# A fused token-mixing, attention and feed-forward kernel on one core: ACT takes a normalisation and four copies, and DVE's and POOL's queues are re-ordered

## The reference

```
q, k, v = token mixing of x inside groups of 16 tokens (Wq, Wkv, biases), 8 tokens out
h = q*scale + softmax(q*scale @ k) @ v                       # (64, 128, 192)
h = h + attention(layernorm(h))    # 12 heads, 3 key/value heads, 64 wide, rope, softmax, Wo
h = h + gelu(layernorm(h) @ W_in.T + b) @ W_out              # 768 hidden
```

## Time and profile before

| | |
|---|---|
| time, median of 3 runs | 1117.43 us (1113.86 to 1119.33) |
| the profiled execution: its own time, its span | 1116.1 us, 1114.3 us |
| busy: PE, DVE, ACT, POOL | 985.3, 797.4, 654.4, 699.8 us |
| share of the span: PE, DVE, ACT, POOL | 88%, 72%, 59%, 63% |
| mean granted TensorE clock | 0.969 of full |

### The profile page before, as it was taken

One profiled execution on the slowest core, in us unless ns is written; L12 is line 12 of the kernel. 1 busy time (PEld: TensorE's weight loads), 2 busy tenths in 40 slices (PEclk: granted clock), 3 DMA queues, 4 the chain that ended last, 5 costly groups with the idle time before them and its releaser, 6 DMA issues. The chain is left out here.

```text
span 1114.3 us, 25412 instructions
## 1 busy us (share of the span) xinstructions
PE 985.3 (88%) x7360; PEld 843.2 (76%) x7360; DVE 797.4 (72%) x1935; ACT 654.4 (59%) x2402; POOL 699.8 (63%) x1063
## 2 busy tenths in 40 slices
PE   3678999999999999999999999999999999999877
PEld 2557778887777887877778787788787787878765
DVE  2677777778778777877777767877777777787751
ACT  2336655665665566566557566556566655756651
POOL 0566576666667666666766656766666676666660
PEclk7779999999999999999999999999999999999998
DMA  5043433344443334444333444333434333443331
GB/s 171 20 132 114 139 96 114 102 124 128 131 130 96 118 97 133 122 137 122 96 108 108 134 125 126 96 118 96 139 120 139 111 107 107 111 139 120 120 105 31
DMA packets 139936, 127.69 MB, mean 115 GB/s; under 512 B 30480, under 2 KB 123024, under 8 KB 139920
## 3 DMA queue, kind: packets, MB, share of 16 engines
q1 hardware_dynamic: 137632, 124.29, 37.5%
q10 hardware_dynamic: 2288, 3.21, 0.8%
HBM read 70.83 MB, written 56.62 MB: 114 GB/s over the span
## 5 line engine op out<-in xcount | busy, mean ns | idle before, releaser
L302 ACT ACTIVATE E<-ring,m_neg 128x128 f32<-128x128 f32 x768 | 271.1, 401 | 13.8 <-DVE m_neg L507 13.8
L402 POOL TENSOR_TENSOR E<-E,e_rcp 128x512 f32<-128x512 f32 x192 | 200.7, 1052 | 95.2 <-DVE e_rcp L527 92.5
L394 POOL TENSOR_TENSOR qkT<-rot_c,rot_s 128x256 f32<-128x256 f32 x256 | 188.1, 735 | 20.1
L518 DVE STREAM_TRANSPOSE EB<-E 128x512 f32<-128x512 f32 x192 | 134.5, 700 | 75.0 <-POOL E L402 75.0
L302 ACT ACTIVATION_READ_ACCUMULATOR E<-ring,m_neg 128x1 f32 x768 | 184.8, 241 | 0.0
L689 PE MATMUL bank<-wout_sb,G 128*128 128x192 f32 x768 | 147.8, 330 | 2.6 <-ACT G L367 2.6
L836 PE MATMUL ring<-wo_sb,OT 128*128 128x192 f32 x768 | 139.4, 332 | 10.4 <-ACT OT L310 10.4
L392 POOL TENSOR_TENSOR rot_s<-rot_s,rope_qs 128x256 f32<-128x256 f32 x192 | 141.0, 734 | 10.8 <-DVE rot_s L495 10.8
L836 PEld LDWEIGHTS ring<-wo_sb,OT 128*128 128x128 f32 x768 | 126.7, 192 | 24.4 <-issue 24.4
L689 PEld LDWEIGHTS bank<-wout_sb,G 128*128 128x128 f32 x768 | 125.3, 192 | 4.3 <-ACT G L367 3.1
L507 DVE TENSOR_REDUCE m_neg<-ring 128x4 f32<-128x512 f32 x192 | 125.6, 682 | 2.2 <-PE ring L708 2.2
(11 more groups left out here) (130 smaller groups left out, 2610.1 us busy)
## 6 DMA issues: line engine op xcount, KB each, us to landing
spill<-EB SPq DMA_DIRECT2D x64, 512.0 KB, 2.7
ET<-spill SPq DMA_DIRECT2D x256, 128.0 KB, 2.8
spill<-EB SPq DMA_DIRECT2D x64, 256.0 KB, 2.0
ET<-spill SPq DMA_DIRECT2D x256, 64.0 KB, 2.3
x_sb<-in_x_dram SPq DMA_DIRECT2D x64, 192.0 KB, 2.5
out_dram<-out_sb SPq DMA_DIRECT2D x64, 96.0 KB, 2.3
x_sb<-in_x_dram SPq DMA_DIRECT2D x64, 64.0 KB, 2.2
w_raw<-in_w_att_dram ACTq DMA_DIRECT2D x2, 608.0 KB, 5.2
```

What stands on the lines that cost most here:

```text
L302: last = nc.scalar.activation(E[:, a, s * P:(s + 1) * P], RING[a][:, s * P:(s + 1) * P], ACT.Exp, bias=m_neg[:, a, s:s + 1], accum_out=e_s ...
L394: nc.gpsimd.tensor_tensor(qkT[:, b, :, a], rot_c[:, b, :, a], rot_s[:, b, :, a], ALU.add).then_inc(q_out, 1)
L402: nc.gpsimd.tensor_tensor(e, e, r, ALU.mult).then_inc(prob_out, 1)
L518: nc.vector.transpose(EB[:, a, s0 * P:(s0 + heads) * P].rearrange("p (j h c) -> p h j c", j=NB, h=heads)[:, h0:h0 + REP], E[:, a, 512 * g: ...
```

## The change

ACT writes `hn` of sequence 0 at the start of its step, as rs * h2 + off, with off = -mean * rs from one more small POOL instruction (`off2`). ACT also makes the four copies `h_cur[0]`, `h_wait`, `v_late` and `h_cur[1]` that POOL made. In DVE's queue `normalise(..., 0)` is gone; `h_next` and its statistics stand ahead of the first block transpose; the residual sum and statistics of sequence 1 stand behind the first block transpose and ahead of the second; two of the three `key_max(1)` banks stand behind the `HL` and result instructions. In POOL's queue the last rotation precedes the first `probs`, and `ve1`/`rs1` precede `probs(0, 2)`, which still precedes `rstd2(..., 1)`. On PE `probs_v(0)` stands ahead of `x_turned`, and on ACT `heads_out(0)` ahead of `XH`.

```diff
 # ACT
+                if ffn:
+                    act.wait_ge(ln2_off, p)
+                    need(act, hT_mm, p - 1)
+                    nc.scalar.activation(hn[:, 0, 0:D], h2[:, 0, :], ACT.Identity, scale=rs2[:, 0:1], bias=off2[:])
+                    nc.scalar.activation(hn[:, 0, D:DP], h2[:, 0, P:D], ACT.Identity, scale=rs2[:, 0:1],
+                                         bias=off2[:]).then_inc(hn_out[0], 1)
+                if att:
+                    act.wait_ge(h_out, p + 1)
+                    need(act, h2_out, 2 * p - 1)
+                    nc.scalar.copy(h_cur[0][:], h_next[:, 0, :]).then_inc(h_kept[0], 1)
+                    nc.scalar.copy(h_wait[:], h_next[:, 1, :]).then_inc(h_moved, 1)
...
                     score_exp(0, 2)
+                    act.wait_ge(v_out, p + 1)
+                    need(act, pv_mm, 4 * p)
+                    nc.scalar.copy(v_late[:], v_tok[:, 1]).then_inc(v_kept, 1)
+                    act.wait_ge(h_moved, p + 1)
+                    need(act, h2_out, 2 * p)
+                    nc.scalar.copy(h_cur[1][:], h_wait[:]).then_inc(h_kept[1], 1)
...
                         score_exp(1, k)
+                    heads_out(0, p)
                 if tok:
                     act.wait_ge(xT_mm, n + 1)
...
-                if att:
-                    heads_out(0, p)
 # POOL
+                    if a == 0:
+                        wait_apart(pool, pool_passed, (ln2_rs, done))
+                        nc.gpsimd.tensor_scalar(off2[:], mv2[:, a, 0:1], rs2[:, a:a + 1], -1.0,
+                                                ALU.mult, ALU.mult).then_inc(ln2_off, 1)
...
-                    for i in range(3):
+                    for i in range(4):
                         rotated(1, i, i + 5)
-                    (copies h_cur[0], h_wait)
                     probs(0, 0, p)
-                    rotated(1, 3, 8)
                     probs(0, 1, p)
-                    probs(0, 2, p)
-                if ffn:
-                    rstd2(2 * p, 1)
                 if tok:
                     (ve1, rs1)
                 if att:
-                    (copies h_cur[1], v_late)
+                    probs(0, 2, p)
+                if ffn:
+                    rstd2(2 * p, 1)
 # DVE
-                    normalise(h2, mv2, rs2, hn, 0).then_inc(hn_out, 1)
...
                     sums_inverted(0, 0, p)
-                    blocks_turned(0, 0, p)
-                    sums_inverted(0, 1, p)
                 (h_next, its bn_stats)
+                if att:
+                    sums_inverted(0, 1, p)
                 (its bn_aggr)
+                if att:
+                    blocks_turned(0, 0, p)
                 if ffn:
                     dve.wait_ge(h_kept[1], p)
                     attention_added(1, 2 * p)
+                    attention_stats(1, 2 * p)
                 if att:
                     blocks_turned(0, 1, p)
                     sums_inverted(0, 2, p)
-                if ffn:
-                    attention_stats(1, 2 * p)
-                if att:
                     blocks_turned(0, 2, p)
                 (normalise sequence 1)
-                    key_max(1, (0, 1))
+                    key_max(1, (0,))
                 (HL, ffn_result)
-                    key_max(1, (2,))
+                    key_max(1, (1, 2))
 # PE
                     ffn_first()
+                if att:
+                    probs_v(0, p)
                 if tok:
                     x_turned()
                 if att:
-                    probs_v(0, p)
                     output(0, p)
```

More of the change, by code:

```diff
@@ L150, in program @@
         st2, mv2, ve2, rs2 = sb("st2", [P, 2, 6]), sb("mv2", [P, 2, 2]), sb("ve2", [P, 2]), sb("rs2", [P, 2])
-        hn = sb("hn", [P, 2, DP])
+        hn, off2 = sb("hn", [P, 2, DP]), sb("off2", [P, 1])
         HH, HL = sb("HH", [P, 2, 2, P], F32R), sb("HL", [P, 2, 2, P], F32R)
@@ L184, in program @@
         y_mm, h2_out, h2_copied = sem("y_mm"), sem("h2_out"), sem("h2_copied")
-        ln2_st, ln2_mv, ln2_ve, ln2_rs, hn_out = (
-            sem(n) for n in ("ln2_st", "ln2_mv", "ln2_ve", "ln2_rs", "hn_out"))
+        ln2_st, ln2_mv, ln2_ve, ln2_rs, ln2_off = (
+            sem(n) for n in ("ln2_st", "ln2_mv", "ln2_ve", "ln2_rs", "ln2_off"))
+        hn_out = [sem("hn_out0"), sem("hn_out1")]
         hT_mm, HH_out, HL_out = sem("hT_mm"), sem("HH_out"), sem("HL_out")
@@ L409, in step @@
                         rotated(0, i, i + 1)
-                    for i in range(3):
+                    for i in range(4):
                         rotated(1, i, i + 5)
-                    wait_apart(pool, pool_passed, (h2_out, 2 * p - 1), (h_out, p + 1))
-                    nc.gpsimd.tensor_copy(h_cur[0][:], h_next[:, 0, :]).then_inc(h_kept[0], 1)
-                    nc.gpsimd.tensor_copy(h_wait[:], h_next[:, 1, :]).then_inc(h_moved, 1)
                     probs(0, 0, p)
-                    rotated(1, 3, 8)
                     probs(0, 1, p)
-                    probs(0, 2, p)
-                if ffn:
-                    rstd2(2 * p, 1)
                 if tok:
@@ L530, in attention_added @@
                     dve.wait_ge(y_mm, done)
+                    if a == 0:
+                        need(dve, hn_out[0], (done - 1) // 2 if isinstance(done, int) else p)
                     nc.vector.tensor_tensor(h2[:, a, :], ATT_Y, h_cur[a][:], ALU.add).then_inc(h2_out, 1)
@@ L560, in step @@
                     v_out_of_psum()
-                if ffn:
-                    dve.wait_ge(ln2_rs, 2 * p - 1)
-                    need(dve, hT_mm, p - 1)
-                    normalise(h2, mv2, rs2, hn, 0).then_inc(hn_out, 1)
                 if tok:
@@ L592, in step @@
                                             ALU.add).then_inc(h_out, 1)
-                if tok:
                     dve.wait_ge(h_out, n + 1)
@@ L596, in step @@
                         nc.vector.bn_stats(st1[:, a, :], h_next[:, a, :]).then_inc(ln1_st, 1)
+                if att:
+                    sums_inverted(0, 1, p)
+                if tok:
                     wait_apart(dve, dve_passed, (ln1_st, 2 * n + 2))
@@ L611, in step @@
                     dve.wait_ge(ln2_rs, 2 * p)
-                    normalise(h2, mv2, rs2, hn, 1).then_inc(hn_out, 1)
+                    need(dve, hT_mm, p - 1)
+                    normalise(h2, mv2, rs2, hn, 1).then_inc(hn_out[1], 1)
                 if att:
-                    key_max(1, (0, 1))
+                    key_max(1, (0,))
                 if ffn:
@@ L814, in hn_turned @@
                 def hn_turned():
-                    pe.wait_ge(hn_out, 2 * p)
+                    pe.wait_ge(hn_out[0], p)
+                    pe.wait_ge(hn_out[1], p)
                     if tok:
```

## The result

The changed kernel takes 1099.13 us (median of 4 runs, 1095.57 to 1100.08). The kernel before takes 1115.99 us over its 4 runs of the same comparison. The ratio is 0.984, with a 95% interval of 0.9805 to 0.9876: 1.6% faster. The profiled execution took 1100.08 us, its span is 1098.3 us.

A forecast was written before the change was run, and what follows sets the result against it. PE's own work plus its waits for t_a, hn and output(0) bound the step. 0.34 + 0.34 - 0.12 = 0.56 us, 16.2 us in 29 steps plus 0.3 in the drain, gave 1100.9; predicted 1100.5, range 1091 to 1112.

The forecast's parts named there:

- my sum: Whole kernel: 0.56 us a step, 16.2 us in 29 steps, giving 1100.9 us to compare; chance 0.50.
- t_a and the mask add: Front of the step: DVE's mask add 0.6 us earlier at most, t_a 0.56; PE's 0.43 us wait for t_a goes.
- The DVE distances: Middle of DVE's queue: 3.74 us from h_next to sums_inverted(0, 2); hn starts 2.14 us after that reciprocal.
- The gain at hn: Middle of the step: hn of sequence 1 comes 0.34 us earlier; PE's wait for it grows from 1.58 to 1.67 us.
- my ceiling of 2.35 us a step: PE's three idle times, before t_a, hn and output(0): the most the change can win, 68 us in 29 steps.
- Its cause: DVE: h_next, no longer behind sums_inverted(0, 1), waits for tok_h instead; sums_inverted(0, 2) starts 0.35 us earlier.
- output(0), 0.34 us: End of the step on PE: x_turned fills the wait for ACT's copy of OT before output(0), winning 0.34 us.
- The gelus, 0.12 us: ACT's gelus become late, so PE waits 0.09 to 0.15 us at the token-mixing products; taken as 0.12.
- The ET reload: Before the second half of probs_v(0) on PE: the reload lands with about 0.3 us of slack, so it is free.
- The clock: PE's granted clock: five of 29 steps stay at reduced clock, each losing 1.3 us.
- The slower rival: The longer wait before the hn transposes lets PE's clock fall every step: 31 us more, 1132 us; chance 0.08.
- The weak side: POOL: sequence 1's statistics come a microsecond earlier, but rstd2 still cannot pass probs(0, 2).

The follow-up runs named there:

- e5: Changed kernel with eight x_sb products first on PE and the gelu wait moved behind them, ahead of the four x2_sb products; 1093.39 us, ratio 0.9803.
- e1: Kernel before with only hn of the first sequence moved from DVE to ACT (off2 on POOL), all orders and POOL copies kept; 1101.09 us, ratio 0.9824.
- e3: Changed kernel with the middle of DVE's and POOL's queues put back in the old order; 1096.39 us, ratio 0.9768.
- e9: e3 with e5's late wait for the gelus; 1092.48 us, ratio 0.9787.
- e4: Changed kernel with only the end order put back: x_turned ahead of probs_v(0) on PE, heads_out(0) behind XH on ACT; 1103.7 us, ratio 0.9851.
- e6: e5 with rstd2(1) ahead of probs(0, 2) on POOL and the second sequence's normalisation ahead of the third block transpose on DVE; 1067.23 us, ratio 0.9569.
- e10: e9 with e6's edit to rstd2 on POOL and the normalisation on DVE; 1119.12 us, ratio 1.0012.
- e7: Changed kernel with one more unused 192-column copy on POOL ahead of rstd2 of the second sequence; 1121.66 us, ratio 1.0058.
- e11: e6 with rstd2(1) also ahead of ve1 and rs1 on POOL; 1086.53 us, ratio 0.9722.
- e8: Changed kernel with one more unused 192-column copy on ACT right ahead of the gelu table load; 1106.05 us, ratio 0.9904.

## Why the prediction came out right, and where its steps did not

The time, 1099.1 us against 1100.5 (my sum gave 1100.9), and the step, 0.53 us less against 0.56, were right. Most of the terms were not.

- **t_a and the mask add.** Right. With the gelu stop out of the way (e5) the add stands at 10.52 in the step against 11.13, the 0.6 us of the sum.
- **The DVE distances.** Right: 3.78 us measured for 3.74, and 2.13 us for 2.14 from there to `hn`.
- **The gain at hn, 0.34 us.** Too small. PE's `hn` transposes stand at 22.53 in e5 against 22.96, 0.43 us. I had taken the stop for `t_a` at the 0.43 us of idle time; `tok_h` on PE moved by 0.57 us (14.97 against 15.54 in e5). A stop of PE costs more than the idle time in its row, so my ceiling of 2.35 us a step was too low as well. PE is ready for `hn` 0.72 us earlier (20.66 in e5 against 21.38), not 0.43; that is why the wait is 1.87 us and not within my 1.6 to 1.8.
- **Its cause.** Wrong. I put it down to `h_next` leaving its place behind `sums_inverted(0, 1)`, and never worked out when the old order would have `hn` with exponentials 0.56 us earlier. e1, e3 and e9 show: at the same time as in the new order. Moving `hn` of the first sequence to ACT was the whole of this term.
- **output(0), 0.34 us.** Too small by the same error: 0.43 us (e4).
- **The gelus, 0.12 us.** Named, but too small: 0.33 us (e5). I computed the gelus' end nearly right; but the gains at `hn` and at `output(0)` were each 0.09 us larger, so PE came 0.18 us earlier than in my sum, and the stop again cost more than its idle time. The end order is worth 0.10 us a step in this kernel, and 0.43 without the stop for the gelus (e4 against e5).
- **The ET reload.** Right: no wait in the full steps of the changed kernel; it appears in e6, where `hn` is earlier.
- **The clock.** Right in count, five of 29. The slower rival had a real mechanism that did not act at 1.87 us and did at 2.02 and 2.16 (e10, e7); even then it took 19 of 29 steps and not all.
- **The weak side.** Right, and the most useful sentence: `rstd2` could not pass `probs(0, 2)`. e6 shows what that hid.

The errors were of opposite sign: 0.43 + 0.43 - 0.33 is 0.53, mine was 0.34 + 0.34 - 0.12. That it fitted is partly luck. Which part of the change collects how much was not foreseen.

## What to carry to other kernels

When a change moves work off a queue and re-orders it as well, work out the old order with the new times too; here the move was 0.42 us, the re-ordering of the middle 0 and that of the end 0.10. A re-ordering that makes a result early is worth something only if the consumer's queue can take it early: look at what stands ahead of it there, and at what the freed engine will run beside. And before removing a wait of PE, look at the next semaphore PE reaches: here the gelus took back three quarters of the gain, and placing eight independent products ahead of their wait returned it.

## What the runs showed of the hardware

The clock of PE went with the length of a wait that recurs in every step. With 1.14 us ahead of the `hn` transposes no full step of 29 had a granted clock under 1.00 (e6), and none in e11 with 0.28 us there and 1.26 us ahead of `HL`; with 1.58 to 1.88 us it was three to eight of 29 (before, after, e1 to e5, e8, e9); with 2.02 and 2.16 us 19 of 29 (e10, e7). The step's length does not explain it (e8 against e7), and inside the middle group the count does not follow the wait. Such a step is 0.6 to 1.4 us longer. The page "TensorE: Matmul & The Clock Gate" of the Trainium skill (HAM oscillation) describes a kernel in which a recurring wait for DMA, about 3 to 5 us by the page, brings the slow clock back at every tile. The waits here are shorter, 1.58 to 2.16 us, and the trace agrees only in part: some steps fall and others, with the same wait, don't. To call my slower rival the case by that page went too far. Between 1.14 and 1.58 us and between 1.88 and 2.02 us I measured nothing, and why one step falls and the next doesn't was not tried.

A stop of PE costs more than the idle time in its row. The stop of 0.35 us ahead of `output(0)` makes a difference of 0.43 us (e4 against the changed kernel). The stop for the gelus has 0.09 us of idle time and costs 0.33 (e5). The rows show where: without a stop PE's products start 0.12 us apart though each lasts 0.28 (L685), an overlap of 0.16 us. At a stop it is lost, and 0.16 + 0.09 are the 0.25 us by which the first product starts later. Then the first four products take 0.71 us instead of 0.61. Why these four take longer was not tried.
